# State space layer: the root of the norms as a power on GpSimd

## The reference, cut to what matters

```python
def rmsnorm(x, w):
    return x * jax.lax.rsqrt(jnp.mean(x * x, axis=-1, keepdims=True) + EPS) * w
Bm = rmsnorm((x @ WB.T).reshape(B_, L, H, N), Bn_w) + B_bias
Cm = rmsnorm((x @ WC.T).reshape(B_, L, H, N), Cn_w) + C_bias
Bm, Cm = rope(Bm, theta_cumsum), rope(Cm, theta_cumsum)
h = at * h + bt * outer(B_prev, x_prev) + gt * outer(Bt, xt)   # per step
yt = jnp.einsum('bhn,bhnp->bhp', Ct, h)
y = y * jax.nn.silu(z)
return y @ Wout.T
```

## Time and profile before

| | |
|---|---|
| median of 3 runs | 1853.73 us (1852.46 to 1959.34) |
| profiled execution | 1853.81 us, span 1852.1 us |
| granted TensorE clock, mean | 0.911 |
| PE busy | 1535.7 us, 83% |
| DVE busy | 1137.4 us, 61% |
| ACT busy | 861.6 us, 47% |
| POOL busy | 499.4 us, 27% |
| the loop of 32 blocks | from about 1468 to 1783 us |

### The profile page before, as it was taken

The page is one execution under the profiler, slowest core; times in us unless marked ns, Lnnn a source line. Parts: engine busy times, 40 slices in busy tenths (PEclk is TensorE's granted clock), DMA queues, the critical chain, the costliest instruction groups (busy, mean ns, idle before and its releaser), DMA issues. The chain is left out here.

```text
span 1852.1 us, 25357 instructions
## 1 busy us (share of the span) xinstructions
PE 1535.7 (83%) x8808; PEld 1095.0 (59%) x8808; DVE 1137.4 (61%) x2329; ACT 861.6 (47%) x1936; POOL 499.4 (27%) x515
## 2 busy tenths in 40 slices
PE   7869988599968895746999999999976588888868
PEld 5644444367645783644777777777742256555557
DVE  5778889256746444653456644445339678888833
ACT  2558889211335321222334433344324577888821
POOL 2350000000000030004342233224000287888820
PEclk9978999689979997577999999999979889999979
DMA  3007999455040101030000000000022232323010
GB/s 125 1 1 146 182 184 182 139 175 173 1 84 13 52 1 35 15 118 1 1 1 1 2 1 1 1 1 1 1 87 79 74 98 69 99 73 97 7 41 34
DMA packets 190491, 110.89 MB, mean 60 GB/s; under 512 B 150121, under 2 KB 166505, under 8 KB 189468
## 3 DMA queue, kind: packets, MB, share of 16 engines
q1 hardware_dynamic: 190364, 109.26, 22.6%
HBM read 75.41 MB, written 0.26 MB: 41 GB/s over the span
## 5 line engine op out<-in xcount | busy, mean ns | idle before, releaser
L2850 POOL TENSOR_TENSOR a_t<-a_t,a_bias_ring 128x512 f32<-128x512 f32 x64 | 128.2, 2022 | 131.3 <-DVE a_t L2922 131.2
L210 PE MATMUL banks<-a_w_ring,x_normed_T 128*128 128x512 f32 x320 | 152.2, 616 | 13.5 <-DVEq L2896 6.0
L670 DVE TENSOR_REDUCE x_row_max<-banks 128x1 f32<-128x512 f32 x248 | 152.1, 680 | 13.9 <-PE banks L364 13.7
L573 ACT ACTIVATE x_v_full<-banks,x_neg_max,x_q_scale 128x1024 int16<-128x1024 f32 x128 | 153.3, 1202 | 14.3 <-DMA x_v_full<-x_v_full 5.7
L2195 PE MATMUL banks<-x_v,x_expsT 128*128 128x128 f32 x1088 | 148.6, 277 | 10.7 <-ACT x_expsT L2353 5.9
L2195 PEld LDWEIGHTS banks<-x_v,x_expsT 128*128 128x128 f32 x1088 | 134.0, 192 | 15.3 <-ACT x_expsT L2353 7.3
L2473 DVE TENSOR_REDUCE x_small<-banks 128x1 f32<-128x2048 f32 x32 | 73.3, 2292 | 86.9 <-PE banks L2176 86.9
L2280 POOL TENSOR_TENSOR x_t<-x_t 128x512 f32<-128x512 f32 (+1 forms) x48 | 54.4, 1134 | 260.6 <-DVE x_t L2455 260.6
L2176 PE MATMUL banks<-x_kT,x_qT 128*128 128x512 f32 x256 | 118.9, 608 | 4.7 <-ACT x_exps L2335 4.7
L364 PE MATMUL banks<-x_kT_parts,x_qT_int 64*128 64x512 bf16 x512 | 105.2, 409 | 5.2 <-DVE x_row_max L670 2.7
L210 PEld LDWEIGHTS banks<-a_w_ring,x_normed_T 128*128 128x128 f32 x320 | 60.4, 197 | 80.8 <-issue 68.4
(11 more groups left out here) (533 smaller groups left out, 3608.4 us busy)
## 6 DMA issues: line engine op xcount, KB each, us to landing
a_w_ring<-in_L_attn_WB_T SPq DMA_DIRECT2D x16, 512.0 KB
a_w_ring<-in_L_attn_WC_T SPq DMA_DIRECT2D x16, 512.0 KB
f_w_gate_up<-in_L_ffn_gate_up SPq DMA_DIRECT2D x18, 352.0 KB
ctx_tokens<-in_ctx SPq DMA_DIRECT2D x16, 256.0 KB, 5.8
a_w_ring<-in_L_attn_Wth_T SPq DMA_DIRECT2D x8, 512.0 KB
a_bias_ring<-in_L_attn_B_bias_perm SPq DMA_DIRECT2D x16, 256.0 KB
a_bias_ring<-in_L_attn_C_bias_perm SPq DMA_DIRECT2D x16, 256.0 KB
f_w_down<-in_L_ffn_down SPq DMA_DIRECT2D x18, 176.0 KB
```

The lines of the kernel that those rows point to most:

```text
L210: last = nc.tensor.matmul(out, lhsT, rhs, start=(i == 0), stop=(i == len(pairs) - 1))
L573: nc.scalar.activation(eb[:, q % RING], k.ps[:, 2 + 2 * (q % 2):4 + 2 * (q % 2), :].rearrange("p a n -> p (a n)"), ACT.Exp, bias=nb[:, v % ...
L670: nc.vector.reduce_max(mx[:, u % 2, i:i + 1], k.bank(MBANK[m % 3]), AX.X).then_inc(s.max_taken, 1)
L2850: last = nc.gpsimd.tensor_tensor(a, a, bring[:, i % RB, j], ALU.add).then_inc(s.bias_used, 1)
```

## The change

GpSimd computes (mean + EPS) to the power of minus one half in one instruction and writes it where the reciprocal stood; ScalarE's square root and VectorE's reciprocal go. A constant tile of minus one half is filled ahead of the loop. GpSimd's root of block n + 1 stands at the end of its iteration n, behind the combine of block n - 1; the signals `var_ready` and `std_ready` keep their names, and VectorE waits for `std_ready` where it did.

```diff
+        neg_half = sb("minus_half", [P, 2 * HG])
 ... (ScalarE)
-                def root(n):
-                    r = n % 2
-                    act.wait_ge(s.var_ready, n + 1)
-                    nc.scalar.activation(st[:, r, 2], st[:, r, 1], ACT.Sqrt).then_inc(s.std_ready, 1)
                 squares(0)
-                root(0)
...
                     if n < NU:
                         decays(n)
-                    if n + 1 < NU:
-                        root(n + 1)
 ... (GpSimd)
-                pool.wait_ge(s.masks_ready, 3)
+                nc.gpsimd.memset(neg_half[:], -0.5).then_inc(s.masks_ready, 1)
+                pool.wait_ge(s.masks_ready, 4)
                 pool.wait_ge(s.ww_ready, 1)
+                def root(n):
+                    pool.wait_ge(s.var_ready, n + 1)
+                    nc.gpsimd.tensor_tensor(st[:, n % 2, 3], st[:, n % 2, 1], neg_half[:], ALU.pow).then_inc(s.std_ready, 1)
+                root(0)
                 for n in range(NU + 2):
...
                         last.then_inc(s.added, 1)
+                    if n + 1 < NU:
+                        root(n + 1)
 ... (VectorE)
                         dve.wait_ge(s.std_ready, n + 1)
                         if n >= 2:
                             dve.wait_ge(s.roped, n - 1)
-                        link(nc.vector.reciprocal(st[:, r, 3], st[:, r, 2]))
```

## The result

The changed kernel takes 1918.32 us (median of 4 runs) against 1854.47 us for the kernel before on the same chip: ratio 1.0348, 95% interval 1.0328 to 1.0368. It is 3.5% slower; 1917 us was forecast. One of the four runs of the kernel before (1959.34 us) and one of the kernel with the root behind the factor (5110.21 us, further down) were far slower than the others of the same kernel; they count in the medians, and the ratios leave them out. The profiled execution took 1918.94 us, with a span of 1916.9 us.

The account below looks back on a forecast made before the run. A ring of waits over two iterations, with no engine full, was taken to bound the loop. A new 11.48 us ring against 9.47 gave 60.3 us, plus 3.2 us: 1853.8 + 63.5 = 1917 us, range 1893 to 1936.

Parts of the forecast that it names:

- The ring: State space loop: root, release, scaling to bias, bias to combine, and combine follow one another each block, 11.48 us against 9.47.
- release: Hand-over from GpSimd's finished root to VectorE's scaling, put at 0.10 us, between 0.03 and 0.15.
- The sum: Loss over the loop: 60.3 us for 30 iterations plus 3.2 us for block 0 to 1, together 63.5 us.
- The freed time: ScalarE's and TensorE's time freed in the loop becomes idle time outside the ring; both priced at nothing.
- half covered: ScalarE's table load ahead of the exponential was half hidden, since the exponential also waits for the decay product.
- a thin case: With the rotation stretched, VectorE's variance comes before the combine ends if two products take under 1.5 us; otherwise some tenths.
- The cheap power: Rival: GpSimd's power costs 0.2 us like a plain operation, ring 10.05 us, about 1872 us; cheap rival 11%.
- The faster one: Rival: ScalarE alone sets the pace and GpSimd follows, an iteration falls to 8.2 us, total 1816 us; 4%.
- TensorE's clock: Rival: less busy, TensorE falls in clock and comes back into the ring, costing 14 us, about 1931 us; 12%.
- VectorE's wait for the power: Sign in the changed profile: VectorE waits for GpSimd's power some 2 to 3 us each time.
- which of bias and rotation gets through first: GpSimd's bias and VectorE's rotation: 4.70 us from bias start to combine start was assumed, whichever gets through first.

Follow-up runs that it names:

- the kernel with the root behind the factor: Changed kernel with GpSimd's root placed behind the past factor instead of ahead of it in its queue; 1955.08 us, ratio 1.0538 to the kernel before.
- the old place: Kernel before with ScalarE's square root replaced by a square at its place, so no table load in the loop; 1835.67 us, ratio 0.9886.
- the kernel with the multiplication: Changed kernel with GpSimd's power replaced by a plain multiplication by minus one half in the same place; 1872.67 us, ratio 1.0091 to the kernel before.
- logarithm and exponential: Kernel before with ScalarE's root as exp(-0.5 ln v) at its place and no reciprocal on VectorE; 1899.89 us, ratio 1.0237.
- the root ahead of the combine: Changed kernel with GpSimd's root between bias and combine; expected about 1887 or about 1950 us, measured 1933.01 us, ratio 1.0428 to the kernel before.
- two moves of a few lines: Kernel before with ScalarE's root ahead of the decay factors (1839.35 us), then also VectorE's variance ahead of its two products (1834.2 us, ratio 0.9894).
- half a rotation: Changed kernel with VectorE's rotation done for B alone, three of six products left out; 1878.14 us, ratio 1.0128 to the kernel before.

## Why the prediction was right, step by step

- **The ring, 11.48 us forecast, 11.42 measured.** Power 1.63 and release 0.10, against 1.68 together; scaling to bias 2.31 against 2.30; bias to combine 4.70 against 4.72; combine 2.74 against 2.72. The two durations of the same operation on 1 and 4 columns gave the third one to 0.01 us. (The prediction speaks of 48 powers of 128x4; there are 40, and 8 of 128x1.)
- **The sum, 63.5 us.** From block 1 to 31 the scaling takes (1818.49 - 1475.93) / 30 = 11.42 us against 9.47, so 58.5 us. Block 0 to 1 takes 6.43 us, 3.1 more than before. The first scaling is 0.7 us later. Together 62.3 of the 64.8 us by which the span grew; the last 2.5 us lie behind block 31 and were put at nothing. That the total is right to 1.3 us is in part luck: 1.8 us too many for the ring stand against 3.2 us that were put at nothing.
- **The freed time is worth nothing in the new ring.** Shown from both sides: 111 us less busy time on ScalarE and VectorE and no gain, and about 20 us from the loads if the root's place is kept. The prediction called the load ahead of the exponential half covered; it was covered but for 0.17 us.
- **Place and duration both count.** With 0.2 us in the root's place and no load per block, the old place gives 1836 us and the new one 1873, so the place costs some 37 us; the power's 1.64 us in place of 0.20 cost another 46. Moving the root by one instruction in the same queue costs 35 to 37 us.
- **The variance has enough cover.** It was priced at nothing, with a thin case if GpSimd got through first. The power waited for it only once, ahead of the loop; in the rows shown it is done at 1654.29, 2.7 us before the power.
- **The rivals.** The cheap power was priced at 1872 us; the kernel with the multiplication gave 1872.67, so the price was right and only its condition false. The faster one asked for cover for the scaling; GpSimd has 1.26 us of it and waits 1.10 more. TensorE's clock: 0.95 in 1576 to 1763 us against 0.98. In some blocks TensorE is at its lower level (the decay product takes 1.91 us at 1659.16 against 1.02 at 1647.01, and ScalarE's exponential waits 2.75 us for it instead of 1.11), but the round stays at 11.42, so the clock stays out of the ring.
- **What was wrong.** VectorE's wait for the power was put at 2 to 3 us; it is 4.24. I had not gone through what VectorE still has to do: its rotation, products, variance and copy are over at 1654.38, before the combine is. It changes no term of the sum. And I left open which of bias and rotation gets through first; here it was the rotation in every block from block 1 on, for the two bias adds take 4.75 us in each.

Both expectations on logarithm and exponential failed as told above (two loads came, but not the 1854 to 1865 us named for them), and the two numbers given for the root ahead of the combine lay far apart because that last point was open.

## What to carry to other kernels

An engine's queue is in order, so moving a step to another engine also moves its result behind whatever stands ahead of it there. Before counting what the old engine saves, write down the ring that the step will be in: here a root that served two blocks from ScalarE became one link of four in a row per block. And look whether the same ring can be shortened by order alone: two moves of a few lines gave 1.1%, as much as removing the loads did.

## What was not expected of the hardware

Bias (GpSimd, two inputs from SBUF) and rotation (VectorE, the same) keep each other out, and the one that is out stays out for a whole row of instructions of the other, not for one. In the loops shown, a bias that begins directly behind GpSimd's own last instruction takes 3.05 to 3.14 us and the rotation is stretched; one that begins after a wait for the scaling takes about 4.75 us (3.48 beside half a rotation). The exceptions are a few blocks at the start of a loop. Where a whole rotation lies beside the bias and the combine comes next in the queue, 4.7 us pass from bias start to combine either way. Which instruction begins first does not tell the two cases apart. In the kernel before the rotation's first product began 0.23 us ahead of the bias in both blocks of the earlier trace rows:

```profile
1599.70 0.76 DVE L2936 TENSOR_TENSOR a_r<-a_t,a_cs 128x512 f32<-128x512 f32 x1
...
1609.56 0.68 DVE L2936 TENSOR_TENSOR a_r<-a_t,a_cs 128x512 f32<-128x512 f32 x1
```

At 1599.93 the bias got in behind that one product; at 1609.79 it stayed out until the rotation was over. The Trainium skill (SBUF — State Buffer, Who interferes with whom) states that a VectorE instruction with two inputs in SBUF contends with a GpSimd instruction that reads SBUF, that the contention is an exclusive lock, and, of VectorE's 2-port modes, that whoever issues first holds the shared pair for its whole instruction while the other is fully blocked. The trace agrees on the blocking. It also shows it over rows of up to six instructions, which a lock for one instruction does not explain; why is open.

The power on GpSimd costs 0.56, 1.02 and 1.64 us for 1, 4 and 8 columns, against 0.20 us for a multiplication of the same 128x8: about 0.15 us per column.
